# The score of batches 0 to 14 as three fp16 products, with its low part placed in the vector engine's queue

## The reference

```
h      = gelu(x @ fc1_w.T + fc1_b)                     # 2048 wide
x      = x + concat(h @ fc2_w.T + fc2_b, h @ experts_w[idx].T + experts_b[idx])
attn   = tanh(x @ W1 + b1)                             # 128 wide
score  = attn @ v                                      # one number for each position
p      = softmax(where(mask[type], score, -1e30))      # l<=j, l>=j or l!=j
x      = x + (p @ x) / count(mask)
```

## Time and profile before

| | |
|---|---|
| median of 3 runs | 1361.4 us (1361.34 to 1362.88) |
| the profiled execution: its time | 1360.97 us |
| its span, first to last instruction | 1359.2 us |
| PE busy | 1348.0 us (99%) |
| DVE busy | 1231.0 us (91%) |
| ACT busy | 867.1 us (64%) |

### The profile page before, as it was taken

One profiled execution on the slowest core, in us unless ns is written; L12 is line 12 of the kernel. 1 busy time (PEld: TensorE's weight loads), 2 busy tenths in 40 slices (PEclk: granted clock), 3 DMA queues, 4 the chain that ended last, 5 costly groups with the idle time before them and its releaser, 6 DMA issues.

```text
span 1359.2 us, 22001 instructions
## 1 busy us (share of the span) xinstructions
PE 1348.0 (99%) x8734; PEld 873.0 (64%) x8734; DVE 1231.0 (91%) x2057; ACT 867.1 (64%) x1493; POOL 0.2 (0%) x4
## 2 busy tenths in 40 slices
PE   9999999999999999999999999999999999999998
PEld 4448476584856748566584765848567584765856
DVE  7996889899898998989899898998989999898998
ACT  4867848377583756838477483766938468483753
POOL 0000000000000000000000000000000000000000
PEclk9999999999999999999999999999999999999999
DMA  8411011110201102010020201102010020200001
GB/s 293 150 37 33 0 63 32 42 52 1 78 17 55 40 1 78 17 62 32 20 75 1 72 24 47 48 0 78 17 62 33 8 79 9 67 27 14 25 10 55
DMA packets 29192, 62.98 MB, mean 46 GB/s; under 512 B 5922, under 2 KB 6690, under 8 KB 26658
## 3 DMA queue, kind: packets, MB, share of 16 engines
q1 hardware_dynamic: 28658, 61.05, 13.7%
q10 hardware_dynamic: 432, 0.53, 0.1%
HBM read 44.79 MB, written 16.78 MB: 45 GB/s over the span
## 4 chain that ended last, share of the span: by engine, by line
PE 90%; DVE 7%; ACT 2%; issue 0%; DMA 0%; ACTq 0%; DVEq 0%
PE ps L398 14%; PE ps L400 14%; PE ps L399 14%; PE ps L317 13%; PE ps L319 13%; PE ps L318 13%; PE ps L288 1%; PE ps L435 1%; PE ps L430 1%; PE ps L599 1%; PE ps L426 1%; PE ps L425 1%; PE ps L424 1%; DVE hl L1066 1%; DVE mx L1005 1%; DVE w2l L1066 1%
## 5 line engine op out<-in xcount | busy, mean ns | idle before, releaser
L398 PE MATMUL ps<-hh,w2l 128*128 128x512 f16 x768 | 291.1, 379 | 0.7 <-ACT ps L626 0.7
L399 PE MATMUL ps<-hh,w2h 128*128 128x512 f16 x768 | 291.1, 379 | 0.0
L400 PE MATMUL ps<-hl,w2h 128*128 128x512 f16 x768 | 291.1, 379 | 0.0
L319 PE MATMUL ps<-xh,w1l 128*128 128x256 f16 x960 | 261.7, 273 | 0.0
L318 PE MATMUL ps<-xl,w1h 128*128 128x256 f16 x960 | 261.7, 273 | 0.0
L317 PE MATMUL ps<-xh,w1h 128*128 128x256 f16 x960 | 261.7, 273 | 0.0
L651 ACT ACTIVATE g<-ps,b1s,ds 128x512 f32<-128x512 f32 x240 | 173.5, 773 | 99.5 <-PE ps L319 98.6
L317 PE MATMUL ps<-xh,ch 128*128 128x256 f16 x720 | 196.4, 273 | 0.6 <-ACT ps L626 0.3
L319 PE MATMUL ps<-xh,cl 128*128 128x256 f16 x720 | 196.3, 273 | 0.0
L318 PE MATMUL ps<-xl,ch 128*128 128x256 f16 x720 | 196.3, 273 | 0.0
L1066 DVE SCALAR_TENSOR_TENSOR hl<-g,ix,hh 128x512 f16<-128x512 f32 x244 | 177.2, 738 | 1.6
(11 more groups left out here) (208 smaller groups left out, 2337.9 us busy)
## 6 DMA issues: line engine op xcount, KB each, us to landing
xr<-in_xT SPq DMA_DIRECT2D x62, 256.0 KB, 3.1
er<-in_ew SPq DMA_DIRECT2D x15, 1024.0 KB, 5.5
out<-xr SPq DMA_DIRECT2D x60, 256.0 KB, 2.4
raw<-in_w SPq DMA_DIRECT2D x28, 256.0 KB, 6.0
er<-in_w SPq DMA_DIRECT2D x3, 1024.0 KB, 10.1
xr<-in_ew SPq DMA_DIRECT2D x1, 1024.0 KB, 6.0
out<-er SPq DMA_DIRECT2D x3, 256.0 KB, 2.5
xr<-in_xT ACTq DMA_DIRECT2D x2, 256.0 KB, 5.1
```

The source lines that it names most:

```text
L319: m = mm(to, wl, mh, start=False, stop=c == 1, skip_group_check=True)
L398: mm(po(b, o), wl, hh[:, k, :], start=False, stop=False, skip_group_check=True)
L399: mm(po(b, o), wh, hh[:, k, :], start=False, stop=False, skip_group_check=True)
L400: m = mm(po(b, o), wh, hl[:, k, :], start=False, stop=k == NH - 1, skip_group_check=True)
```

## The change

The score's inputs are split like the others. `v` is loaded as one column (`vcol`), its largest magnitude goes through the chain that makes power-of-two scales (column 17 of the scale tables, made together with batch 1's), and `vh`, `vl` are made from it once, broadcast along 128 columns. For batches 0 to 14 ACT writes the high part of the tanh, times 2^13, into `hh[:, 0, :]`, and DVE the low part into `hl[:, 0, :]`; PE makes three fp16 products, and `keep_score` takes the scale out again. The last batch keeps the fp32 product, for which `avs`, which now shares its memory with `vh` and `vl`, is loaded late. On DVE, `attention_low` stands between `add_second` of pair 0 and the pooling; one pooling step is left ahead of `add_first` of pair 1, and one is moved behind it.

```
         def score(b):
-            e.wait_ge(tanh_done, b + 1)
-            e.wait_ge(av_in, 16)
-            mm(pa, avs[:, :], att, start=True, stop=True).then_inc(score_done)
+            e.wait_ge(atth_done, b + 1)
+            e.wait_ge(vl_done, 1)
+            mm(pa, vl[:, :], hh[:, 0, :], start=True, stop=False)
+            mm(pa, vh[:, :], hh[:, 0, :], start=False, stop=False)
+            e.wait_ge(attl_done, b + 1)
+            mm(pa, vh[:, :], hl[:, 0, :], start=False, stop=True).then_inc(score_done)
...
         e.wait_ge(bound_step, 6)
-        chain_sum(9, hc(1), hc(1) + 3)
+        e.wait_ge(vmax_done, 1)
+        chain_sum(9, hc(1), vc + 1)
...
             act(att, pa, ACT.Tanh, bias=abs_[:, 0:1]).then_inc(tanh_done)
+            e.wait_ge(tanh_done, b + 1)
+            copy(hh[:, 0, :], att, grow[:, 0:1]).then_inc(atth_done)
...
-            copy(sc, pa).then_inc(scored)
+            e.wait_ge(vinv_done, 1)
+            copy(sc, pa, vinv[:, 0:1]).then_inc(scored)
...
+        def attention_low(b):
+            e.wait_ge(atth_done, b + 1)
+            low_part(hl[:, 0, :], att, grow[:, 0:1], hh[:, 0, :]).then_inc(attl_done)
...
         weight_sums(0)
+        e.wait_ge(vcol_in, 16)
+        column(vc, vcol[:, :]).then_inc(vmax_done)
         bounds(1)
...
         expert_low(0, 1)
+        e.wait_ge(vh_done, 1)
+        low_part(vl[:, :], vcol.broadcast_to([A, P]), scale_of(vc), vh[:, :]).then_inc(vl_done)
+        ts(vinv[:, :], ex[:, vc:vc + 1], 2.0 ** -13, None, ALU.mult).then_inc(vinv_done)
         pads()
...
             add_first(b + 1, 0)
             add_second(b + 1, 0)
-            pool(2)
+            attention_low(b)
+            pool(1)
             add_first(b + 1, 1)
-            pool(3)
+            pool(4)
...
-        dma(avs[:, :], av).then_inc(av_in, 16)
+        dma(vcol[:, :], av[:, 0:1], allow_slow_non_contiguous=True).then_inc(vcol_in, 16)
...
                 dma(aws[:, 0:3, :], aw[:, 0:3, :]).then_inc(aw_in, 16)
+                e.wait_ge(score_done, LAST)
+                dma(avs[:, :], av).then_inc(av_in, 16)
```

More of the change, by code:

```diff
@@ L68, in build @@
     aws_at = here()
-    aws, avs = sb("aws", [P, KD, A]), sb("avs", [A, P])
+    aws, avs_at = sb("aws", [P, KD, A]), here()
+    avs = sb("avs", [A, P])
+    vh, vl = (nc.alloc_sbuf_tensor_at(n, [A, P], f16, offset=avs_at + at) for n, at in (("vh", 0), ("vl", 2 * P)))
+    cols = sb("cols", [P, 16])
+    ones, abs_, vcol, vinv, grow, rz = (cols[:, lo:hi] for lo, hi in ((0, 1), (1, 2), (2, 3), (3, 4), (4, 5), (8, 12)))
     early_at = here()
@@ L93, in build @@
     io = sb("io", [P, S], f16)
-    b1s, b2s, ebs, abs_ = sb("b1s", [P, NH]), sb("b2s", [P, 3]), sb("ebs", [P, 2]), sb("abs", [P, 1])
+    b1s, b2s, ebs = sb("b1s", [P, NH]), sb("b2s", [P, 3]), sb("ebs", [P, 2])
     lcol, scol, shift, limit = sb("lcol", [P, 4]), sb("scol", [P, 4]), sb("shift", [P, 4]), sb("limit", [P, B])
-    rz, ones = sb("rz", [P, 4]), sb("ones", [P, 1])
     idxs, pts = sb("idxs", [1, B], i32), sb("pts", [P, B], i32)
@@ L103, in build @@
     oneb = sb("oneb", [P, P], bf16)
-    NC = 17
+    NC = 18
     mx, ex, ix, lift = sb("mx", [P, NC], bf16), sb("ex", [P, NC]), sb("ix", [P, NC]), sb("lift", [P, NC])
-    w1c, w2c = 3, 11
+    w1c, w2c, vc = 3, 11, 17
     def hc(b):
@@ L192, in build @@
         sem(n) for n in ("e0in", "idxin", "ptin", "b1in", "b2in", "awin", "abin", "avin", "ioin", "eyein", "lcolin"))
+    vcol_in, vmax_done, vh_done, vl_done, vinv_done, atth_done, attl_done = (
+        sem(n) for n in ("vcolin", "vmax", "vh", "vl", "vinv", "atth", "attl"))
     (bits_set, summed, tile_done, p1, p5, p6, p7, p3, fc2_done, half_done, attended, score_done, nat_done, cols_done,
@@ L479, in score_half @@
             e.wait_ge(tanh_done, LAST + 1 + v)
+            e.wait_ge(av_in, 16)
             mm(pf[n][:, 0:HALF], avs[:, :], att[:, HALVES[v]], start=True, stop=True).then_inc(score_done)
@@ L878, in scalar_program @@
         split_expert_high(0, 1)
+        e.wait_ge(ix_done, 9)
+        copy(vh[:, :], vcol.broadcast_to([A, P]), scale_of(vc)).then_inc(vh_done)
         split_x_high(1, X11)
@@ L1022, in chain_scale @@
             e.wait_ge(summed, n)
-            e.wait_ge(ones_set, 7)
+            e.wait_ge(ones_set, 8)
             stt(ex[:, lo:hi], pss[:, lo:hi], TINY, lift[:, lo:hi], ALU.max, ALU.mult).then_inc(pss_read)
@@ L1040, in batch_scales @@
         def batch_scales(b):
-            chain_scale(8 + b, hc(b), hc(b) + 3)
+            chain_scale(8 + b, hc(b), hc(b) + 3 if b > 1 else vc + 1)
             fc1_scale(b, 8 + b, 0, PAIRS)
@@ L1287, in vector_program @@
         eng.memset(x5[:, :, KD:KD + 1], 1.0).then_inc(ones_set)
-        for lo, hi, power in ((0, 2, -14), (2, 11, -12), (11, 16, -14), (16, 17, -12)):
+        eng.memset(grow[:, :], 2.0 ** 13).then_inc(ones_set)
+        for lo, hi, power in ((0, 2, -14), (2, 11, -12), (11, 16, -14), (16, 18, -12)):
             eng.memset(lift[:, lo:hi], 2.0 ** power).then_inc(ones_set)
@@ L1390, in vector_program @@
         add_second(1, 0)
+        attention_low(0)
         add_first(1, 1)
```

## The result

| | before | changed |
|---|---|---|
| median of 6 runs each | 1361.45 us | 1372.61 us |
| ratio to before, 95% interval | | 1.0083 (1.0072 to 1.0093) |
| profiled execution: time / span | 1360.97 / 1359.2 us | 1374.21 / 1372.4 us |

The change costs 11.2 us; 11.5 had been forecast. One of the six runs of before took 3685.28 us, and the ratio goes by the others. The profiled execution of the changed kernel lies 1.6 us above its own median, so times along it are compared within an opening and between scores, not at the ends.

The account below looks back on a forecast made before the run. PE was taken to bound the kernel, with DVE next: 1360.97 profiled + 11.3 (14 openings x 0.81) + 0.39 at the start - 0.21 at score 0 = 1372.5, or 1372.9 us as median; range 1367 to 1376.

Parts of the forecast that it names:

- PE's saving, 0.21 a score: At each score on PE: three fp16 products take 0.65 us instead of 0.86 for fp32; 3.2 us over 15 batches if hidden.
- The chain tanh, copy, low part: Ahead of the score: with 0.03 us handovers, low part done at 598.68, wanted at 599.32, so the score waits for nothing.
- DVE's delay, 1.13: At each opening: idle for the high part plus the low part make DVE's following steps 1.13 us later.
- The spare time, 0.32: At pair 6: 0.42 us between add_second's end and product4, less a 0.10 handover, leaves 0.32 to absorb delay.
- The stalls' places: PE waits for add_second in 14 batches: about 0.6 us at pair 1, smaller ones later, some 14 us in all.
- PE's busy time: Over the whole run: PE's busy time falls by about 3 us while the span grows.
- The start, 0.39: On DVE at the start: low part of v and the multiply for vinv add 0.39 us, bounds 0.26 and 0.66.
- The saving at score 0: Score 0, followed by a batch with no pooling in the early cycles, keeps its 0.21 us.
- All hidden: Rival, 8%: PE bounds the kernel and DVE's low part finds room, so it gets faster, 1358.6 us.
- Only pair 1 pays: Rival, 10%: unseen slack lets DVE catch up behind pair 1; 0.40 us a batch, 1367.2 us.
- The clock falls behind the stalls: Rival, 3%: each PE stall brings a microsecond at the lower clock, half of it lost; 7 us over 14, 1380.

Follow-up runs that it names:

- e3: Changed kernel with two pooling steps taken from between add_first and add_second of pair 1 and done behind add_second of pair 7: 1358.84 us, ratio 0.9980.
- e4: Changed kernel with DVE's low part of the tanh behind the first scan instead of ahead of it: 1365.87 us, ratio 1.0033.
- e5: Changed kernel with DVE's low part of the tanh done a second time, into a tile that nobody reads: 1381.84 us, ratio 1.0145.
- e1: Kernel before the change with only the second scan moved behind add_first of pair 1, the score still one fp32 product: 1361.34 us, ratio 0.9999.
- e2: Changed kernel without DVE's low part of the tanh and without the score's third product: 1356.84 us, ratio 0.9965.
- e6: e3 with the start's low part of v and scale multiply moved to where DVE waits for PE: 1358.08 us, ratio 0.9974.

## Why the prediction was right, point by point

- **PE's saving, 0.21 a score.** Right: 0.65 us in the trace, and e3, where nothing hides it, shows 0.22 a distance.
- **The chain tanh, copy, low part.** Right: handovers of 0.03 (602.12 to 602.15, 602.87 to 602.90), the low part done at 603.65, wanted at 604.28. `keep_score` with a scale from a tile takes 0.69, between the 0.60 and the 0.77 that bounded it.
- **DVE's delay, 1.13.** 1.16 measured. e4 takes its two parts to pieces, e5 adds a third, e1 clears the moved scan. The low part takes 603.57 - 602.90 = 0.67 from start to start where it has a follower, not its full 0.75: the rows' price. The prediction told only half of what the Trainium skill says here (VectorE: DVE Perf Modes, "The DRAIN you can't avoid"): the same section adds that "A next op that is not held starts earlier". Here the next one starts 0.08 us ahead of the record's end, which agrees with the addition.
- **The spare time, 0.32.** A little low: the handover is 0.06 at pair 1 (610.29 to 610.35) and at pair 6 (633.61 to 633.67), so 0.36 to spare, and e2 and e4 give the same. 14 x (1.16 - 0.36) = 11.2, where 11.3 had been worked out: the two small errors cancel, which is luck. From score to score the trace has 0.78 on average (82.78 against 81.99), so 14 x 0.78 = 11.0.
- **The stalls' places.** 0.59 at pair 1, where 0.61 had been forecast; the other three waits (pairs 2, 4 and 6) come to about 0.37 by the starts of the matmuls. That is 14 x 0.96 = 13.4 us in all, against some 14.
- **PE's busy time.** The sign was wrong: a fall of about 3 us had been forecast, and it rose by 5.9. Of each batch's 0.96 us of stall only 0.42 shows as idle; the other 0.54 hides in the records, 14 x 0.54 = 7.6 us, and the score's 15 x 0.21 = 3.2 comes off. Most of what is left over comes from the clock at the end of this execution (last section).
- **The start, 0.39.** Measured 0.33 (39.45 against 39.12, under e6). The saving at score 0 came to 82.47 - 82.34 = 0.13, not 0.21; where the rest went is open. With these the sum is 11.0 + 0.33 - 0.13 = 11.2, as the medians have it. None of this can be read from the ends of two profiles. Up to its first score the changed kernel's profile is 1.1 us behind that of before, but e1's, whose start is untouched, is behind by 0.9: in e1 DVE waits for the third piece of the second layer's weights, which in the profile of before had landed in time.

```profile
65.95 2.29 DVE L1005 TENSOR_REDUCE mx<-er 128x1 bf16<-128x2048 f32 x1 [0.87 <-DMA er<-in_w]
```

- **Rivals.** All hidden: refuted by 56 waits. Only pair 1 pays: refuted by the waits at pairs 2, 4 and 6. The clock falls behind the stalls: refuted, 1.00 through the window of the stalls, and the matmuls behind the one at 610.35 keep their 0.11. That rival leaned on a clock of 1.00 beside the kernel's first, slow matmuls; the profile of before has no clock record there (the first begins 4.1 us into the span), so that 1.00 was not a reading.

## What to carry to other kernels

When an engine is 91% busy on average, look for the stretch in which it has no hole and for the deadline at its end: what is added ahead of that stretch costs its time, and the wait for its input, less the smallest spare time at any deadline, and what the other engine saved doesn't come off. To put the new work elsewhere in the stretch gives back the wait at most (e4: 6.7 of 11.2 us); to move as much old work past the last deadline, into a hole, gives back the rest too (e3). If steps of unequal length come from one sequence, a step left out is worth, at each deadline, the step that stood last ahead of it.

## What had not been expected of the hardware

The changed kernel's profiled execution lies 1.6 us above its median. In its last 20 us the granted clock fell from 1.00 to the lower of its two levels for a while, and about the same stretch of the kernel before kept 1.00. Window sums of the changed kernel, then of before (stretch, length, busy time of PE, PEld, DVE, ACT, POOL, clock, transfers); PE is as busy in both by its records, with 33 matmuls in the first, some of them at the lower clock, and 46 in the second:

```profile
1350.00:1360.00 10.00, 8.19 (x33) 5.31 (x32) 9.38 (x16) 7.05 (x11) 0.00 (x0) 0.83 0.01 2
```
```profile
1336.00:1346.00 10.00, 8.20 (x46) 5.50 (x46) 9.58 (x15) 6.57 (x12) 0.00 (x0) 1.00 0.00 0
```

What PE did just ahead was the same too: both kernels have their longest wait there, 1.8 us for `ph` (the earlier trace rows for before), and it ends at 1355.35 in the changed kernel, where the clock falls at 1356.6.

```profile
1355.35 1.20 PE L609 MATMUL ps<-nh,ph 128*128 128x512 f32 x5 [1.81 <-ACT ph L1011]
```

So the drop comes in some executions and not in others, in a tail that all these kernels share: of the nine profiles, those of the changed kernel, e2 and e5 have it. It is far from the stalls that the change brings. From the last of the 15 scores to the end it is 106.37 us in the changed kernel and 103.96 in e3, which has no drop; one opening more accounts for 82.78 - 81.77 = 1.01 of the difference. The 1.4 us left are the price of the drop, and the same sum gives 1.4 for e2 and for e5. The other 0.2 of the 1.6 us, a wait for a load at the start among them, was not taken apart.
